# Five f32r products for the routed down projection, split weights through device memory

## The reference

```python
I, E, TOP_K, IS = 176, 16, 6, 352
scores = jax.nn.softmax(x @ gate_w.T, axis=-1)
topk_w, topk_ids = lax.top_k(scores, TOP_K)
topk_w = topk_w / (topk_w.sum(-1, keepdims=True) + 1e-20)
combine = jnp.einsum('tk,tke->te', topk_w, jax.nn.one_hot(topk_ids, E))
def body(acc, ew):
    w13_e, w2_e, c_e = ew
    return acc + c_e[:, None] * _swiglu(x, w13_e, w2_e), None
out, _ = lax.scan(body, jnp.zeros_like(x), (w13, w2, combine.T))
out = out + _swiglu(x, sw13, sw2)
```

## Time and profile before

| what | us |
|---|---|
| median of 3 runs (lowest, highest) | 726.3 (725.83, 727.24) |
| the profiled execution's own time | 727.58 |
| its span (first to last instruction) | 725.8 |
| PE busy / DVE / ACT / POOL in the span | 657.1 / 410.3 / 375.8 / 400.5 |
| mean granted clock of TensorE | 0.953 |

### The profile page before, as it was taken

How to read it: one execution, slowest core, us unless ns; L and a number is a source line. 1 busy time by engine, 2 the same in 40 slices (tenths; PEclk the granted TensorE clock), 3 DMA queues, 4 the chain that set the end, 5 groups by cost and what they waited for, 6 DMA issues and landing times.

```text
span 725.8 us, 13640 instructions
## 1 busy us (share of the span) xinstructions
PE 657.1 (91%) x4213; PEld 495.9 (68%) x4213; DVE 410.3 (57%) x1138; ACT 375.8 (52%) x902; POOL 400.5 (55%) x413
## 2 busy tenths in 40 slices
PE   8999997999989999966699999999999999998077
PEld 7888996999868987744465665655656656554067
DVE  6878879889788768788523323233232332322255
ACT  3788798989888655243244443444434444343000
POOL 3678778861766410000566666666666666673131
PEclk9999999999999999975799999999999999999588
DMA  8000001260000119300223333233333333331994
GB/s 309 2 1 1 2 1 45 75 191 3 2 1 31 45 45 294 66 12 0 70 90 98 98 94 100 93 98 98 95 101 91 98 98 95 101 96 61 302 348 159
DMA packets 49123, 65.48 MB, mean 90 GB/s; under 512 B 8024, under 2 KB 38880, under 8 KB 48928
## 3 DMA queue, kind: packets, MB, share of 16 engines
q1 hardware_dynamic: 37984, 34.00, 15.3%
q0 software_dynamic: 10656, 30.02, 13.3%
q10 hardware_dynamic: 416, 0.59, 0.2%
HBM read 45.57 MB, written 19.02 MB: 89 GB/s over the span
## 4 chain that ended last, share of the span: by engine, by line
PE 73%; DVE 9%; ACT 5%; SPq 4%; issue 3%; POOL 3%; DMA 2%; DVEq 0%; ACTq 0%; POOLq 0%
PE ps L1464 18%; PE ps L1483 10%; PE ps L1482 7%; PE ps L1456 6%; SPq L483 4%; PE ps L1110 4%; PE ps L1474 3%; PE ps L1316 3%; PE ps L1261 2%; PE ps L1248 2%; PE ps L1237 2%; PE ps L1262 2%; PE ps L1151 2%; PE ps L1277 1%; DVE q L1913 1%
## 5 line engine op out<-in xcount | busy, mean ns | idle before, releaser
L677 POOL DMA_INDIRECT xg<-token_rows,idx x111 | 108.9, 981 | 145.1 <-DVE idx L1940 78.7
L2003 DVE SCALAR_TENSOR_TENSOR sw<-sil,cwt,ps 128x176 f32<-128x176 f32 x111 | 44.1, 398 | 217.7 <-ACT sil L999 217.7
L1464 PE MATMUL ps<-up_w,gT 128*128 x444 | 151.1, 463 | 0.1
L681 POOL DMA_INDIRECT routed<-yb,home x111 | 109.6, 988 | 41.4 <-issue 34.8
L1464 PEld LDWEIGHTS ps<-up_w,gT 128*128 128x128 f32 x444 | 76.2, 192 | 24.6 <-issue 1.4
L1005 ACT ACTIVATE yb<-ps 128x256 f32<-128x256 f32 x111 | 42.6, 384 | 96.7 <-PE ps L1483 96.7
L999 ACT ACTIVATE sil<-ps,zero 128x176 f32<-128x176 f32 x111 | 45.2, 407 | 90.7 <-PE ps L1464 90.7
L1483 PE MATMUL ps<-dn,swT 48*128 x222 | 77.3, 428 | 0.0
L1482 PE MATMUL ps<-dn,swT 128*128 x222 | 66.4, 381 | 0.0
L1483 PEld LDWEIGHTS ps<-dn,swT 48*128 48x128 f32 x222 | 32.7, 184 | 36.8 <-issue 36.8
L1456 PE MATMUL ps<-ident,xg 128*128 128x128 f32 x222 | 48.7, 302 | 5.9 <-DVE x1T L1878 5.9
(11 more groups left out here) (284 smaller groups left out, 1486.5 us busy)
## 6 DMA issues: line engine op xcount, KB each, us to landing
yacc<-routed SPq DMA_DIRECT2D x24, 512.0 KB, 7.5
up_w<-in_moew SPq DMA_DIRECT2D x4, 1408.0 KB, 12.8
wog<-combine SPq DMA_DIRECT2D x2, 1024.0 KB, 6.1
token_rows<-hxb SPq DMA_DIRECT2D x8, 256.0 KB, 2.2
out<-x1T SPq DMA_DIRECT2D x8, 256.0 KB, 3.0
xg<-token_rows,idx POOLq DMA_INDIRECT x111, 2.8
routed<-yb,home POOLq DMA_INDIRECT x111, 2.4
raw<-in_moew SPq DMA_DIRECT2D x3, 384.0 KB, 3.6
```

Of the source, the lines that this page charges most:

```text
L677: po.indirect_dma_start(xg[:, i % XG_BUFS, :], None, hx_d[:, :], bass.IndirectOffsetOnAxis(ap=idx[:, i:i + 1], axis=0)).then_inc(S[f"ld_xg ...
L681: po.indirect_dma_start(y6_d[:, :], bass.IndirectOffsetOnAxis(ap=home[:, k:k + 1], axis=0), yb[:, k % Y_BUFS, :], None).then_inc(S[f"sc{k ...
L1464: last = mm(up_block(j), gT[:, j % 2, kc, :], up_w[:, kc, :, bass.ds(expert[j], 1), :], start=(kc == 0), stop=(kc == KC - 1))
L2003: ve.scalar_tensor_tensor(out=sw[:, j % 2, 0:I], in0=sil[:, j % 2, :], scalar=cwt[:, j % 4:j % 4 + 1], in1=up_block(j)[:, 1, :], op0=ALU.m ...
```

## The change

It does four things.

1. The routed down projection takes five f32r products: high x high, high x low and low x high on the 128 rows, then one on 112 rows whose weights hold the high part of the last 48 rows in rows 0 to 47 and the low part in rows 64 to 111, and low x high on 48 rows. ACT makes `swThi`, DVE `swTlo` (in place of `swT`) and a second copy of 48 columns of `sw`.
2. The down weights are split on POOL, in 8 groups of two experts, between `wlo` and `wog`. SP brings the small rows (`d1raw`), and stores the high part and the 112-row tile to device memory. Buffers are single. In the shared stage POOL brings them back, 2 DMAs after each third of units.
3. In the shared stage the low part `alo` is made by POOL. Some of DVE's routing steps stand earlier.
4. At the end the loads of `yacc` with odd j are issued by ACT, those with even j by SP; POOL's addition goes, and PE sums four terms (0+1, 2+3, 4, 5).

```diff
@@ sync @@
-            down_rows(0, dn0, range(E))
+            down_rows(0, dn0raw, 0, 0, range(E), "ld_dn0")
+            sp.wait_ge(*late("zrow_ok", 2))
+            for g in range(E // EG):
+                experts = range(EG * g, EG * (g + 1))
+                if g:
+                    sp.wait_ge(*late("d1_ok", g))
+                for q in (0, LO1):
+                    down_rows(1, d1raw, EG * g, q, experts, "ld_d1")
+                sp.wait_ge(*late("d0_hi", g + 1))
+                sp.dma_start(dn0_d[:, EG * g:EG * (g + 1), :], d0hi[:, :, :].bitcast(F32)).then_inc(S["st_d0"], 16)
+                sp.wait_ge(*late("d1_ok", g + 1))
+                sp.dma_start(dn1_d[:, EG * g:EG * (g + 1), :], d1[:, :, :].bitcast(F32)).then_inc(S["st_d1"], 16)
...
-            for blk in range(NBLK):
-                sp.wait_ge(S["e_up"], SHARED * (blk + 1))
-                down_rows(1, dn1, range(blk * E // NBLK, (blk + 1) * E // NBLK))
...
-                for j in range(TOPK):
+                for j in range(0, TOPK, 2):
@@ gpsimd @@
+            po.wait_ge(S["f_s7"], 1)
+            po.memset(d1raw[:, :, :], 0.0).then_inc(S["zrow_ok"], 1)
...
+            po.wait_ge(*late("ld_dn0", 16 * len(dn_pieces[0])))
+            for g in range(E // EG):
...
+                if g:
+                    po.wait_ge(*late("st_d0", 16 * g))
+                    po.wait_ge(*late("d0_lo", g))
+                po.tensor_copy(d0hi[:, :, :], dn0raw[:, experts, :]).then_inc(S["d0_hi"], 1)
+                po.wait_ge(*late("d0_hi", g + 1))
+                po.tensor_tensor(dn0lo[:, experts, :], dn0raw[:, experts, :], d0hi[:, :, :].bitcast(F32), ALU.subtract).then_inc(S["d0_lo"], 1)
...
+                po.wait_ge(*late("ld_d1", 16 * pieces_in))
+                if g:
+                    po.wait_ge(*late("st_d1", 16 * g))
+                po.tensor_copy(d1[:, :, :], d1raw[:, :, :]).then_inc(S["d1_hi"], 1)
+                po.wait_ge(*late("d1_hi", g + 1))
+                po.tensor_tensor(d1[LO1:, :, :], d1raw[LO1:, :, :], d1[LO1:, :, :].bitcast(F32), ALU.subtract).then_inc(S["d1_ok"], 1)
...
+            for n in range(NU):
+                po.wait_ge(S["e_hi"], n + 1)
...
+                po.tensor_tensor(alo[:, n % 3, :], pm[:, n % 3, :], ahi[:, n % 4, :].bitcast(F32), ALU.subtract).then_inc(S["e_lo"], 1)
+                if n % SHARED == 0 and n:
+                    down_experts(n // SHARED - 1)
+            down_experts(NBLK - 1)
...
-                po.tensor_tensor(yacc[blk][:, 4, :, :], yacc[blk][:, 4, :, :], yacc[blk][:, 5, :, :], ALU.add).then_inc(S["acc_p"], 1)
@@ scalar @@
+                    ac.activation(swThi[:, j % 2, :, :], turned_block(j), ACT.Copy).then_inc(S["s_hi"], 1)
...
+                for j in range(1, TOPK, 2):
+                    ac.dma_start(yacc[blk][:, j, :, :], routed[:, j, 4 * blk:4 * blk + 4, :]).then_inc(S[f"ld_acc{blk}"], 16)
@@ tensor @@
-                    mm(o, swT[:, j % 2, 0, :], dn0[:, bass.ds(expert[j], 1), :], start=True, stop=False)
-                    mm(o, swT[0:I2, j % 2, 1, :], dn1[:, bass.ds(expert[j], 1), :], start=False, stop=True).then_inc(S["s_dn"], 1)
+                    high, low, at_e = swThi[:, j % 2, :, :], swTlo[:, j % 2, :, :], bass.ds(expert[j], 1)
+                    mm(o, high[:, 0, :], dn0hi[:, at_e, :], start=True, stop=False)
+                    mm(o, high[:, 0, :], dn0lo[:, at_e, :], start=False, stop=False)
+                    mm(o, low[:, 0, :], dn0hi[:, at_e, :], start=False, stop=False)
+                    mm(o, high[0:LO1 + I2, 1, :], dn1[:, at_e, :], start=False, stop=False)
+                    mm(o, low[0:I2, 1, :], dn1[0:I2, at_e, :], start=False, stop=True).then_inc(S["s_dn"], 1)
...
-                        for j in (0, 2, 4):
+                        for j in (0, 2, 4, 5):
@@ vector @@
-                if 1 <= n <= NU:
-                    low(n - 1)
...
+                    ve.scalar_tensor_tensor(out=sw[:, j % 2, P + LO1:P + LO1 + I2], in0=sil[:, j % 2, P:I], scalar=cwt[:, j % 4:j % 4 + 1],
+                                            in1=up_block(j)[:, 1, P:I], op0=ALU.mult, op1=ALU.mult).then_inc(S["s_a"], 1)
...
-                    ve.tensor_copy(swT[:, j % 2, :, :], bank(4 + j % 2)[:, 0:2 * P].rearrange("p (k t) -> p k t", k=2)).then_inc(S["s_aT"], 1)
+                    ve.tensor_tensor(swTlo[:, j % 2, :, :], turned_block(j), swThi[:, j % 2, :, :].bitcast(F32), ALU.subtract).then_inc(S["s_aT"], 1)
```

More of the change, by code:

```diff
@@ L55 @@
 I2 = I - P
+LO1 = 64
+EG = 2
 XG_BUFS, Y_BUFS, ONE_BUFS = 6, 4, 4
@@ L195, in build @@
         assert one_end <= TMP_END and y_end <= end and end + 2 * TPB * D * 4 <= TMP_END
[L196 to L199, removed]
+        (d0hi, d1raw, d1), stage_end = carve(end, [("d0hi", [P, EG, D], F32R), ("d1raw", [LO1 + I2, EG, D], F32), ("d1", [LO1 + I2, EG, D], F32R)])
+        assert stage_end <= TMP_END
+        (gT, sw, swThi, swTlo), k_end = carve(R_k, [
+            ("gT", [P, 2, KC, P], F32), ("sw", [P, 2, 2 * P], F32), ("swThi", [P, 2, 2, P], F32R), ("swTlo", [P, 2, 2, P], F32R)])
+        assert k_end <= R_v
+        q0 = at("q0", [P, 2, TOPK, QW], F16, end)
+        selt = at("selt", [P, NB, E], BF16, end)
+        hits = at("hits", [P, TOPK, QW], F32, yb_at)
         yacc = [at(f"yacc{i}", [P, TOPK, 4, D], F32, (R_wo, R_wo + 24576, R_q, R_q + 24576)[i]) for i in range(NBLK)]
@@ L999, in _ @@
                     ac.activation(sil[:, j % 2, :], up_block(j)[:, 0, :], ACT.Silu, bias=zero[:, :]).then_inc(S["s_sil"], 1)
+                j = i - 2
+                if 0 <= j < NB:
+                    ac.wait_ge(*late("s_at", j + 1))
+                    if j >= 2:
+                        ac.wait_ge(*late("s_dn", j - 1))
+                    ac.activation(swThi[:, j % 2, :, :], turned_block(j), ACT.Copy).then_inc(S["s_hi"], 1)
                 j = i - 3
+                if j == 0:
+                    ac.wait_ge(*late("idx_ok", 2))
                 if j >= 0:
@@ L1005, in _ @@
                     ac.activation(yb[:, j % Y_BUFS, :], bank(6 + j % 2)[:, 0:D], ACT.Copy).then_inc(S["s_y"], 1)
+            for k in range(Y_BUFS):
+                ac.wait_ge(S[f"sc{k}"], 16 * len(range(k, NB, Y_BUFS)))
+            routed = y6_d[0:TOPK * T, :].rearrange("(j t p) d -> p j t d", j=TOPK, p=P)
+            for blk in range(NBLK):
+                for j in range(1, TOPK, 2):
+                    ac.dma_start(yacc[blk][:, j, :, :], routed[:, j, 4 * blk:4 * blk + 4, :]).then_inc(S[f"ld_acc{blk}"], 16)
         @block.tensor
@@ L1836, in _ @@
                     route_probs(0)
+                if s == B:
+                    route_top(0)
+                    route_combine(0)
                 b = s
@@ L1863, in _ @@
                     ve.tensor_scalar(var2[:, b * TPB:(b + 1) * TPB], mv[:, b * TPB:(b + 1) * TPB, 1], LN_EPS, None, ALU.add).then_inc(S["var2"], 1)
-            def low(n):
-                ve.wait_ge(S["e_hi"], n + 1)
-                if n >= 3:
-                    ve.wait_ge(S["e_dn"], n - 2)
-                ve.tensor_tensor(alo[:, n % 3, :], pm[:, n % 3, :], ahi[:, n % 4, :].bitcast(F32), ALU.subtract).then_inc(S["e_lo"], 1)
             def add_y(blk):
@@ L1911, in one_hots @@
                     ve.wait_ge(*late("q_oh", t - 1))
+                elif t == 0:
+                    for k in range(2):
+                        ve.wait_ge(*late(f"st_hx{k}", 8 * B))
                 blocks = iota[:, 0:QW].rearrange("p (o b) -> p o b", o=1).to_broadcast([P, TOPK, QW])
@@ L1930, in selectors @@
                 ve.tensor_tensor(sel[:, :, 1:E], selt[:, :, 1:E], selt[:, :, 0:E - 1], ALU.subtract).then_inc(S["sel_ok"], 1)
-                for k in range(2):
-                    ve.wait_ge(*late(f"st_hx{k}", 8 * B))
-                ve.memset(sw[:, :, I:2 * P], 0.0).then_inc(S["sel_ok"], 1)
             def slot_tokens():
@@ L1986, in _ @@
                     add_y((n - LAG) // SHARED)
-            ve.wait_ge(*late("sel_ok", 3))
+            ve.memset(sw[:, :, I:P + LO1], 0.0).then_inc(S["sel_ok"], 1)
+            ve.memset(sw[:, :, P + LO1 + I2:], 0.0).then_inc(S["sel_ok"], 1)
+            ve.wait_ge(*late("sel_ok", 4))
             for i in range(NB + 2):
```

65 lines of the change are left out of this document (42 added, 23 removed).

## The result

The change made the kernel slower: 741.82 us median of 4 runs (739.46 to 744.21) against 726.77 of 4 runs of before (725.83 to 729.66) on the same chip, a ratio of 1.020 with a 95% interval of 1.017 to 1.023. A second set of five runs gave 742.76 (741.04 to 744.89), ratio 1.022 (1.020 to 1.024). The forecast was 737, 726 to 755. A run over 1.5% above the fastest of its kernel is called slow and left out of medians and ratios; there was one, in e3_low_dve. The profiled execution of after took 740.49 us, its span 738.7, 12.9 more than before.

A forecast was written before the change was run, and what follows sets the result against it. PE's (TensorE's) order of work was taken as nearly the path. 727.6 + 39.3 + 1.5 + 0.15 + 0 - 30 - 0.1 = 738.5 us for the profiled execution; median forecast 737, range 726 to 755.

The forecast's parts named there:

- The middle: Ahead of `w_ok`: the split on POOL, with waits for small loads, delays it from 184.03 to 223.4 us, +39 us.
- Rival (a): Middle: the split hides, only computing counts, delay +20, 718 us; the point is a delay of 28.5; chance 0.11.
- The restart: After standing still in the middle, PE begins at the low clock: +1.5 us (0 to 2.8).
- The routed loop: Five f32r products replace four passes: 0.27 us saved per block, 111 blocks, -30 us.
- rival (b): Routed loop gives little, through the passage to 112 rows: 758 us, much more with exposed weight loads; chance 0.12.
- POOL's 2.56 then takes over: Routed loop: PE's period falls to 2.545 us, so POOL's 2.56 us a block becomes the bound.
- PE a little below full: Sign in the profile after: a routed period of 2.56 us with PE not quite fully busy.
- The shared stage: DVE's relief from 12 subtractions against POOL's subtractions holding up DVE: sum 0, between -2 and +5 us.
- the 0.75: Shared stage: gain given back by two DVE subtractions that stood ahead of PE's wait for `alo`, in us.
- the +2: Shared stage: POOL's subtraction hits DVE's chain about four times, each with 0.5 us more than it gives.
- the 1.2: Shared stage: gain in us from two subtractions fewer on DVE's chain before the tables.
- The tail: Bound by DMA; two queues 0 to -0.3, DVE -2.0, PE +1.9: together -0.1 us, up to +4 with low clock.

The follow-up runs named there:

- e3_low_dve: The change with the low part of the shared activations made by DVE again; 737.38 us, median of three runs, ratio 1.015 to before.
- e1_one_load: The change without the small down loads of groups 1 to 7, which split group 0's rows again; 728.15 us, ratio 1.001 to before.
- v1_packed: The change with down weights split as they lie in memory, loaded early, three buffers for the high part; 697.30 us, ratio 0.958 to before.
- e2_full_rows: The change with the last of the five products on 112 rows instead of 48; 738.36 us, ratio 1.015 to before.
- v1_old_tail: v1_packed with the merge as before: all yacc loads on SP, POOL's addition, three terms on PE; 699.06 us, ratio 0.961 to before.

## Why the prediction was right, point by point

*The middle.* Shown. `w_ok` was forecast at 223.4 and came at 221.57 and 223.8 us. Groups of 6 and 4 loads were forecast at 6.7 and 5.8 us and took 6.6 and 5.7 to 6.0. The start was sized too late by 1.3 us: SP began its loads at 143.24, no later than before, so POOL's new memset wasn't on its path. That a group waits for its own small loads was shown by taking them away (e1_one_load), that PE waits for POOL by the same run and by v1_packed. Rival (a) had the right break-even, a delay of 28.5: with the small loads gone the delay is 27.3 and the kernel is level with before.

*The restart* was sized at 1.5, "a part of the restart waits for others anyway"; it cost 2.7. That term was too small. The granted clock was 0.50 from 222 to 226 us and 0.66 from there to 230, and what was hoped of the waits of others doesn't show; without the stop, in v1_packed, the stretch is 10.7 us again, as before. The stretches of after, columns as in the earlier trace rows:

```profile
222.00:226.00 4.00, 3.21 (x23) 3.15 (x24) 1.21 (x2) 0.95 (x2) 2.96 (x3) 0.50 0.00 0
226.00:230.00 4.00, 4.00 (x42) 3.91 (x41) 1.94 (x4) 2.63 (x5) 2.27 (x2) 0.66 0.00 0
```

*The routed loop.* -30 was forecast, -29.3 came. The 112-row product costs no passage, so rival (b) falls, and no weight load is exposed. But "POOL's 2.56 then takes over", and with it the sign "PE a little below full", isn't what the trace shows: PE was busy for 50.00 of 50.00 us. The two bounds, PE's 2.545 and POOL's 2.56, are so near to each other that the size came out all the same, which is luck. e2_full_rows tells them apart at the start of the loop: with POOL's program as it was, its blocks come every 2.22 us where those of after take 2.56, so there PE is the bound. Later both are at their floors, POOL's at 2.57.

*The shared stage.* 0 was forecast, within -2 and +5; it cost 2.7 in the profiled execution. The term was the sum of a gain and a contention. The first down product comes 0.7 us earlier (20.4 instead of 21.1) where the clock stays; that this is the 0.75 forecast for PE's wait for `alo` is not shown by itself. The stretch behind it is 1.8 to 2.0 longer than with the low parts on DVE or in before, with three collisions of 0.8 to 1.1. That is the +2 that was forecast for them; the 1.2 that was taken off beside it for DVE's shorter chain was the wrong part, and in some measure counted twice, since the +2 was already what a hit costs "more than it gives". The other 1.6 of the 2.7 go with the clock, which the forecast didn't have.
The Trainium skill ("SBUF — State Buffer", Who interferes with whom) says that a DVE instruction with two inputs in SBUF contends with a GpSimd instruction that reads SBUF; the trace agrees where they meet, 1.95 instead of 0.85 us. Here they met three times in twelve of POOL's subtractions.

*The tail* was -0.1 and is -0.7 by the table, of which some 0.8 are the loop's shorter period in the last three blocks (3 x 0.27), so about even. The additions and products of the last merge take 2.36 and 7.41 us in v1_packed (2.5 and 7.5 forecast; by the rate named there, 0.684 us for 512 columns, the additions would be 2.7). The split of issue over two queues brought no block sooner: from the last routed up product to DVE's additions of the four blocks it is 19.9, 29.0, 38.4 and 47.5 us in v1_packed, 19.5, 28.5, 37.5 and 46.8 with one queue in v1_old_tail.

*The sum* was 738.5 for the profiled execution against 740.49; the terms missed by -1.8 (middle), +1.2 (restart), +2.7 (shared stage), +0.7 (loop) and -0.7 (tail and reload), which is +2.1. In size the misses add up to some 7 us, so a part of the closeness is luck. The median lay 4.8 above the forecast 737, since it was set 1.3 below the profiled execution as in before, while after's median lies 1.3 above its own.

## What to carry to other kernels

Before work is put on an engine with idle time, look at what stands behind it in that engine's order and who waits there: 18.6 us of idle time covered a third of 56 us of new work and waiting, and the rest stopped TensorE one to one, eating a gain of 29 us in the loop. A single-buffered chain of small transfers is paid for in round trips, so split data as it lies and let the later load make the layout. A faster stage of a pipeline is worth no more than the next engine's floor, so read that floor first.

## What the runs showed of the hardware

- A product on 48 rows, behind one on 112 and ahead of one on 128, costs 0.19 us on the way in and 0.15 on the way out; with 112 rows in its place both are gone.
- Five f32r products of 256 columns, each with its own weights, follow each other every 0.12 us, though one weight load shows as 0.19 us: loads overlap with each other as well as with products. PE's weight loads in after:

```profile
402.19 0.19 PEld L1559 LDWEIGHTS ps<-dn0lo,swThi 128*128 128x128 f32 x1
402.31 0.19 PEld L1560 LDWEIGHTS ps<-dn0hi,swTlo 128*128 128x128 f32 x1
```

- The granted clock in the same instructions fell or stayed from one trace to the next (0.53 and 1.00 at 272 us); the stretch is 1.6 us longer in all six traces where it fell; what tips it is open.
